# Part writes, first maxima and the eight places of the lead: a new order of work ahead of the first attention block and in the tail

## The reference, cut to what matters

```
h   = layernorm(x)
q   = h Wq + bq            k = (h Wk + bk) Wl + bl       v = (h Wv + bv) Wl + bl
16 heads of width 8:  out = softmax(q k^T / sqrt(8)) v
x1  = x + layernorm(out Wo + bo)
h1  = layernorm(x1);  the row before each row is mixed in by mu_r, mu_k
y   = x1 + layernorm( sigmoid(xr W_r) * ( relu(xk W_k)^2 W_v ) )
```

## Time and profile before

| | |
|---|---|
| three runs | 260.94 us median (260.84 to 261.55) |
| the profiled execution | 260.82 us, of it 259.0 us from the first to the last instruction |
| mean granted TensorE clock | 0.994 of full speed |
| busy: PE, DVE, ACT, POOL | 94%, 78%, 68%, 38% of the span |

### The profile page before, as it was taken

The page is one execution under the profiler, slowest core; times in us unless marked ns, Lnnn a source line. Parts: engine busy times, 40 slices in busy tenths (PEclk is TensorE's granted clock), DMA queues, the critical chain, the costliest instruction groups (busy, mean ns, idle before and its releaser), DMA issues.

```text
span 259.0 us, 4266 instructions
## 1 busy us (share of the span) xinstructions
PE 243.8 (94%) x1359; PEld 91.7 (35%) x1359; DVE 201.7 (78%) x363; ACT 176.5 (68%) x344; POOL 97.2 (38%) x228
## 2 busy tenths in 40 slices
PE   8999979999999999999999999999999999899980
PEld 3554432223222242234322522343224323332560
DVE  3795988778888799879699899796898997721665
ACT  2565868778776866787677767866777677686122
POOL 5948772010101105641216255512153545117322
PEclk9999999999999999999999999999999999999997
DMA  5345765303030303030304130303031000000101
GB/s 162 86 141 158 210 177 168 87 9 93 2 95 2 92 9 87 4 89 4 91 4 94 42 91 4 91 2 94 4 91 42 3 2 0 7 0 0 43 0 41
DMA packets 13816, 15.68 MB, mean 61 GB/s; under 512 B 3153, under 2 KB 11346, under 8 KB 13794
## 3 DMA queue, kind: packets, MB, share of 16 engines
q1 hardware_dynamic: 13218, 15.15, 21.6%
q10 hardware_dynamic: 576, 0.26, 0.4%
HBM read 11.01 MB, written 4.19 MB: 59 GB/s over the span
## 4 chain that ended last, share of the span: by engine, by line
PE 78%; DVE 10%; issue 3%; POOL 3%; ACT 2%; DMA 1%; POOLq 0%; DVEq 0%; ACTq 0%
PE psO L1327 23%; PE psB L1315 21%; PE psA L1296 18%; DVE mx L957 6%; PE psM L1210 3%; PE psM L1216 2%; PE psM L1196 2%; DMA x_all<-in_L_attn_x_dram 1%; PE psO L1234 1%; PE psM L1243 1%; POOL mm L509 1%; PE psM L1276 1%; PE psA L1196 1%; PE psB L1505 1%; PE psM L1256 1%
## 5 line engine op out<-in xcount | busy, mean ns | idle before, releaser
L957 DVE TENSOR_REDUCE mx<-psA 128x2 f32<-128x1024 f32 x128 | 151.1, 1219 | 31.0 <-PE psA L1296 30.6
L809 ACT ACTIVATE pT<-psB 128x512 f32<-128x512 f32 x244 | 132.9, 596 | 39.9 <-PE psB L1315 39.6
L1315 PE MATMUL psB<-QS,KS 75*128 75x512 bf16 x244 | 92.6, 383 | 0.8 <-ACT pT L809 0.3
L1296 PE MATMUL psA<-KS,QS 72*128 72x512 bf16 x256 | 86.7, 379 | 0.4 <-DVE mx L957 0.3
L1327 PE MATMUL psO<-pT,Vg 128*32 128x512 f32 x512 | 68.2, 604 | 0.4
L1315 PEld LDWEIGHTS psB<-QS,KS 75*128 75x128 bf16 x244 | 23.2, 97 | 82.8 <-ACT pT L809 60.8
L1296 PEld LDWEIGHTS psA<-KS,QS 72*128 72x128 bf16 x256 | 24.8, 98 | 18.9 <-DVE mx L957 3.0
L509 POOL TENSOR_TENSOR mm<-mx,one 128x16 bf16<-128x16 f32 x16 | 3.5, 218 | 39.4 <-DVE mx L957 39.4
L1327 PEld LDWEIGHTS psO<-pT,Vg 128*32 128x32 f32 x512 | 10.2, 107 | 18.2 <-issue 13.4
L549 POOL TENSOR_TENSOR Vg<-v_st,one 128x128 f32<-128x128 f32 x16 | 6.3, 402 | 26.4 <-PE psO L1327 26.4
L1196 PE MATMUL psA<-warm 128*128 128x512 bf16 x33 | 9.9, 448 | 1.6 <-DVE warm L921 1.2
(11 more groups left out here) (183 smaller groups left out, 265.4 us busy)
## 6 DMA issues: line engine op xcount, KB each, us to landing
KS<-k_scr SPq DMA_DIRECT2D x45, 96.0 KB
QS<-q_scr SPq DMA_DIRECT2D x15, 288.0 KB
k_scr<-kp SPq DMA_DIRECT2D x12, 128.0 KB, 2.3
q_scr<-qp SPq DMA_DIRECT2D x12, 128.0 KB, 2.4
x_all<-in_L_attn_x_dram SPq DMA_DIRECT2D x4, 256.0 KB, 3.4
out_dram<-out_sb SPq DMA_DIRECT2D x3, 256.0 KB, 2.3
KS<-k_scr SPq DMA_DIRECT2D x6, 48.0 KB
QS<-q_scr SPq DMA_DIRECT2D x2, 144.0 KB
```

Of the source, the lines that this page charges most:

```text
L809: nc.scalar.activation(pT[:, n % 2, i, :], score_bank(n, i, last), ACT.Exp, scale=SCALE).then_inc(e_rdy, 1)
L957: nc.vector.tensor_reduce(out=mx[:, g % 2, c:c + 2], in_=psA[:, u, :, :], axis=AX.X, op=ALU.max).then_inc(a_max, 1)
L1296: score = nc.tensor.matmul(psA[:, u, j, :], QS[g][0:ROWS, h, P * t:P * (t + 1)], KS[g][0:ROWS, h, :], start=True, stop=True)
L1315: nc.tensor.matmul(score_bank(n, i, last), KS[g][0:KEXP, i, P * t:P * (t + 1)], QS[g][0:KEXP, i, :], start=True, stop=True).then_inc(b_rdy, 1)
```

## The change

The SP queue writes part 1 and part 2 of k for batch 0 ahead of part 1 and part 2 of q. `split_qk` is cut in two functions: `rests_qk` (rest q, rest k) and `thirds_qk` (third q, third k); POOL now runs rests of batch 2, the split of the first maxima, thirds of batch 2, rests and thirds of batch 3. On ACT, `take_xT(3)` and `take_q(3)` stand earlier, `second_k(2)` later, and `take_first_maxima` stands ahead of `take_k(3)`. On PE, `v` of batch 1 moves from ahead of the lead into its first place, `xT` of batch 2 goes to (0, 1), `xT(3)` and `v(2)` change places, `k(3)` goes from (3, 1) to (4, 0), `job_m(0)` from ahead of the pair (4, 1) to behind it; `keep_warm(8)` becomes `keep_warm(3)`; the wait for all v copies goes into block 0. In the tail PE makes product r of half 0 ahead of product k of half 1, ACT's copies go in the order x1T(0), k(0), x1T(1), r(0), k(1), r(1), and the last `keep_warm(2)` becomes `keep_warm(1)`. The loads keep their order.

```diff
--- before.py
+++ after.py
@@ -437,9 +437,12 @@
 
             for b in range(2, NB):
                 load_x(b)
-            for i in range(PARTS):
-                write_k(0, i)
-                write_q(0, i)
+            write_k(0, 0)
+            write_q(0, 0)
+            write_k(0, 1)
+            write_k(0, 2)
+            write_q(0, 1)
+            write_q(0, 2)
             sp.wait_ge(s_pad, NG)
             sp.wait_ge(k_wr[0], 16 * PARTS)
             load_heads(0, 0, 0, ld_first)
@@ -527,7 +530,7 @@
                 pool.wait_ge(r_sem, b + 1)
                 nc.gpsimd.tensor_tensor(nb[:, :], nm[:, :], rs[:, :], ALU.mult).then_inc(b_sem, 1)
 
-            def split_qk(b):
+            def rests_qk(b):
 
                 for full, rest, parts, taken, r1, p2 in ((qf, qr, qp, q_tak, q_r1, q_p2),
                                                          (kf, kr, kp, k_tak, k_r1, k_p2)):
@@ -535,6 +538,8 @@
                     pool.wait_ge(p2, b)
                     nc.gpsimd.tensor_tensor(rest[:, :], full[:, :], parts[:, b % 2, 0, :],
                                             ALU.subtract).then_inc(r1, 1)
+
+            def thirds_qk(b):
                 for rest, parts, p1, p2 in ((qr, qp, q_p1, q_p2), (kr, kp, k_p1, k_p2)):
                     pool.wait_ge(p1, b + 1)
                     nc.gpsimd.tensor_tensor(parts[:, b % 2, 2, :], rest[:, :], parts[:, b % 2, 1, :],
@@ -587,13 +592,16 @@
             link(last)
             link(nc.gpsimd.memset(xs[:, 0:1], 0.0))
             rstd_x(3)
-            split_qk(1)
+            rests_qk(1)
+            thirds_qk(1)
             pool.wait_ge(v_tak, 1)
             for g in range(NG):
                 v_group(0, g, True)
-            split_qk(2)
+            rests_qk(2)
             split_maxima(0, 0)
-            split_qk(3)
+            thirds_qk(2)
+            rests_qk(3)
+            thirds_qk(3)
 
             def batch(b, first, last):
                 if not first:
@@ -773,9 +781,9 @@
                 second_part(b, kr, kp, k_r1, k_p1)
 
             for take, b in ((take_q, 1), (take_k, 1), (take_v, 1), (second_q, 1), (take_xT, 2),
-                            (second_k, 1), (take_q, 2), (take_k, 2), (take_v, 2), (second_q, 2),
-                            (take_xT, 3), (second_k, 2), (take_q, 3), (take_k, 3),
-                            (take_first_maxima, 0), (take_v, 3), (second_q, 3), (second_k, 3)):
+                            (second_k, 1), (take_q, 2), (take_k, 2), (take_xT, 3), (take_v, 2),
+                            (second_q, 2), (take_q, 3), (second_k, 2),
+                            (take_first_maxima, 0), (take_k, 3), (take_v, 3), (second_q, 3), (second_k, 3)):
                 take(b)
 
             def take_o(n, done):
@@ -865,10 +873,10 @@
                                      ACT.Relu).then_inc(z_relu, 1)
 
             z_take_x1T(0)
+            z_take_k(0)
             z_take_x1T(1)
-            z_take_k(0)
+            z_take_r(0)
             z_take_k(1)
-            z_take_r(0)
             z_take_r(1)
 
             for u in range(2):
@@ -1355,25 +1363,22 @@
                              stop=True).then_inc(s_bo, 1)
             job_q(1)
             job_k(1)
-            job_v(1)
-            keep_warm(8)
+            keep_warm(3)
             pe.wait_ge(s_wtc, 3)
 
-            LEAD_JOBS = {(0, 0): (("xT", 2),),
+            LEAD_JOBS = {(0, 0): (("v", 1),),
+                         (0, 1): (("xT", 2),),
                          (1, 0): (("q", 2),),
                          (1, 1): (("k", 2),),
-                         (2, 0): (("v", 2),),
-                         (2, 1): (("xT", 3),),
+                         (2, 0): (("xT", 3),),
+                         (2, 1): (("v", 2),),
                          (3, 0): (("q", 3),),
-                         (3, 1): (("k", 3),),
+                         (4, 0): (("k", 3),),
                          (5, 0): (("v", 3),)}
             for a in range(LEAD):
                 for u in range(2):
                     if a == 0 and u == 1:
                         pe.wait_ge(s_boc, 1)
-                    if a == GH and u == 1:
-                        pe.wait_ge(xT_tak, NB)
-                        job_m(0, psB[:, 0, :].bitcast(bf16))
                     if (a, u) in ((1, 0), (4, 0)):
 
                         pe.wait_ge(a_max, a * 2 + (u - 1))
@@ -1383,7 +1388,9 @@
 
                     for job, e in LEAD_JOBS.get((a, u), ()):
                         {"xT": job_xT, "q": job_q, "k": job_k, "v": job_v}[job](e)
-            pe.wait_ge(v_tak, NB)
+                    if a == GH and u == 1:
+                        pe.wait_ge(xT_tak, NB)
+                        job_m(0, psB[:, 0, :].bitcast(bf16))
             pe.wait_ge(m_tak, 1)
 
             def batch(b, first, last):
@@ -1417,6 +1424,8 @@
 
                     for_exponentials(0)
                     for_maxima(0, 0)
+                    if first and n == 0:
+                        pe.wait_ge(v_tak, NB)
                     for_exponentials(1)
                     for_maxima(0, 1)
                     jobs(n, 0)
@@ -1486,7 +1495,7 @@
                                       (z_1st, 2 * HALF, 4), (z_1rs, 1, 2)):
                 keep_warm(fill, psM[:, :])
                 pe.wait_ge(step, count)
-            keep_warm(2, psM[:, :])
+            keep_warm(1, psM[:, :])
 
             def z_x1T(u):
                 pe.wait_ge(z_1h, u + 1)
@@ -1510,8 +1519,8 @@
             pe.wait_ge(z_w, 3)
             z_product_k(0)
             z_x1T(1)
+            z_product_r(0)
             z_product_k(1)
-            z_product_r(0)
             for u in range(2):
                 pe.wait_ge(z_ka, u + 1)
                 z_product_by_tile(u, "f", (lambda t: kact[:, P * t:P * (t + 1)], w_mix[:, 2, :]),
```

## The result

The changed kernel takes 264.66 us (median of 6, 263.6 to 266.44) against 261.36 for the kernel before (6 runs, 260.84 to 261.65). The ratio on record is 1.0111, with a 95% interval of 1.0061 to 1.0161 (the quotient of these medians would be 1.0126). Forecast was 260.95, range 260.2 to 261.6. The profiled execution took 263.6, its span 261.8, at a mean clock of 0.979 (before: 260.82, 259.0, 0.994).

The account below looks back on a forecast made before the run. PE, busy for 45.37 of 45.70 us from 45.3 us on, was taken as the bound; lead +0.33 and tail -0.3 gave 0.0 on 260.82, and with the median 0.12 above it 260.95 us, range 260.2 to 261.6.

Parts of the forecast that it names:

- the third rival: PE's empty queue from 19.35 to 20.87 us halves its clock in the lead: +4, 265 us; chance 0.04.
- the sum: Whole kernel: +0.33 from the lead and -0.3 from the tail make 0.0 on the profiled execution.
- The row that was to clear the rival: End of the kernel: clock stays 1.00 through 2.60 us without PE work, cited against a fall in the 1.5 us gap.
- the rule that it was set against: The Trainium skill's rule for PE's clock: half rate is the default and activity releases it.
- Start of the lead: First pair of the lead starts at 20.87 us instead of 21.59, 0.72 sooner through k's earlier write.
- Eighth maximum: DVE's eighth maximum in the lead ends 10.8 us after the first pair, at 31.65, 0.9 sooner.
- PE's first 75-row product: PE's first second-pass product follows the eighth maximum by 4.22 us, at 35.9 instead of 36.75.
- First exponential: ACT's first exponential, held by POOL's four operations behind the split, starts at 37.96 us instead of 37.39, 0.57 later.
- Into the blocks: From the third exponential on the delay is 0.33 us, handed to PE's product at 41.03; the lead costs +0.33.
- Tail: End of the kernel: earlier transpose and earlier product r(0) let DVE start f_sb sooner, -0.3 us.
- the exponentials are not held: First exponential follows the maxima without waiting for POOL, at 36.5 us; median 259.5 us; chance 0.09.

Follow-up runs that it names:

- e1: Changed kernel with six filling products after the lead's last pair and four in block 0: 260.70 us, ratio 0.9917 to the kernel before.
- e7: Changed kernel with second_q(3) and second_k(3) behind the exponentials of blocks 0 and 1, six fillings after the lead's last pair: ratio 0.9949.
- e9: Kernel before with POOL's new order alone: 265.0 us, ratio 1.0136.
- e3: Kernel before with the tail's part of the change alone: 260.8 us at full clock, 265.0 us in low runs.
- e4: Changed kernel with second_q(3) and second_k(3) behind the exponentials of blocks 0 and 1: 259.95 us at full clock, 263.9 us in low runs.
- e14: Kernel before with four fillings ahead of job_m(0), two after the lead's last pair, and the tail's part of the change: 260.9 us, ratio 0.9982.
- e5: Changed kernel with the six fillings after the lead's last pair alone: 261.2 us at full clock, 264.4 us in low runs.
- e2: Changed kernel with keep_warm(3) at the start back to keep_warm(8): 266.1 us, all runs low.
- e6: Changed kernel with the four fillings inside block 0 alone: 260.6 us at full clock, 262.7 us in low runs.

## Why the prediction was wrong

**The step that failed** is the third rival, "PE's clock falls", and with it the sum, in which waits count as time only. The prediction looked for the fall at one place, PE's empty queue from 19.35 to 20.87, and gave it 0.04. The sum itself had forecast PE ready for block 0 at 35.9 and its exponential at 37.96; that is two waits of PE between the lead's last pair and block 1, and no step asked what they do to the clock. The fall behind them cost 3.1 us in the profiled run, as e1 shows. The rival's own price, 265 us, lies near the measured 264.66 by luck: it put the half rate into the lead and made the eighth maximum late, and that maximum was on time.

The row that was to clear the rival was misread. PE does nothing from 253.2 to 255.8 at clock 1.00, but right behind it the same trace has

```profile
255.90:259.00 3.10, 0.00 (x0) 0.00 (x0) 0.62 (x2) 0.00 (x0) 0.09 (x1) 0.50 0.29 85
```

So that idle stretch did cost the clock, only later, as it fell at 39.4 behind waits that had begun at 34.7, and the row speaks for the rule that it was set against. A clock that is still full during an idle stretch doesn't show that it will stay full behind it. The Trainium skill (TensorE: Matmul & The Clock Gate, A second HAM failure mode: psum-queue depth-cycling) tells of a kernel in which short idle pieces between groups of products made the clock go up and down. The traces here agree in so far as the clock fell behind pieces of at most 1.34 us in the changed kernel's profiled run; it fell once there and didn't go up and down.

**The other steps**, by the trace and e1 (the same program, filled):

- Start of the lead: 20.62, forecast 20.87 (bounds 20.2 to 21.03). The write of k's last part went out 0.74 sooner (12.86 + 1.24 - 0.52 = 13.58 against 14.32), not 0.56, and the KS loads followed it by 2.58, not 2.83, so the QS load moved by 1.0, not 0.72. Right in kind, 0.25 short.
- Eighth maximum: 10.78 after the first pair, forecast 10.8. Right.
- PE's first 75-row product: 36.03, forecast 35.9. That is near by luck: the eighth maximum ended at 31.40, 0.25 sooner than forecast, but the product followed it by 4.63, not by the 4.22 carried over from the kernel before; in e7 it followed by some 5.9.
- First exponential: 37.58, forecast 37.96: 0.25 from the start, 0.1 from POOL's operations, which start 1.11 apart, not 1.15. Right as a mechanism, and e9 shows the term by itself.
- Into the blocks: in e1 the product of 41.03 stands at 40.97, a gain of 0.06 where a loss of 0.33 was summed; the same 0.4 us as in the line above.
- Tail: -0.23 in the traces of the changed kernel and e3, forecast -0.3. Right.
- At full clock the whole is -0.4 us (e1), forecast 0.0, within what such a measurement can tell.
- The rival "the exponentials are not held" would have been -1.4; e4's two runs at full clock are -1.2.
- The size of the loss against the kernel before has luck in it too: by their times its first 6 runs all kept the clock, and of the next 113 runs 47 did not. In e1's series its median is 263.83, not 261.

**Open.** Why a given run falls and the next one doesn't; whether the filling inside block 0 really does more than the longer one ahead; why the fall lasts 6.7 us in one profile and 13.6 in another. Whether e1, the whole change with fillings, beats e14, its tail and fillings alone, isn't settled either: they ran in different series, at 260.7 and 260.9 us, so a gain from the new lead is not shown.

## What to carry to other kernels

When a change moves a wait onto PE, price it twice: its time, and the clock behind it, which can cost more where PE is the bound (here 2.6 us of waits brought a fall that cost 3.1 us, and e1, with the waits filled, is no slower than the kernel before). Look at every idle piece in front of the PE-bound stretch, not only at the longest, and fill each that can't be removed; ten filling products were worth 4 us of the median here. A few runs at full clock prove nothing of a kernel: the first 6 of the kernel before were all full by their times, of the next 113 forty-seven were not.

## What the runs showed of the hardware

- The granted clock is 1.00 or 0.50 in every trace, but for windows that hold a change. A fall at the start of the blocks lasted 6.7 us (changed kernel, e4), 10.1 or 10.2 (e5, e9) or 13.6 (e2), although PE was busy again: 6.70 of 6.70 us, 10.20 of 10.20, 12.59 of 13.60.
- The clock fell behind idle pieces of PE of 0.84 and 0.29 us (e5), and held behind 1.77 and 0.34 (e6).
- A DMA of 12 KB, issued among loads and writes of 96 to 288 KB, took from 2.36 us (kernel before) to 4.0 us (e7) from its issue to the product that waited for it. Against the kernel before, its issue 1.1 us sooner gave PE 0.7 us in the changed kernel; in e7 it was issued 1.0 us sooner and PE went on 0.6 us later.
